# Two half-full key blocks made as one across the array's columns and rows, and a last key moved to VectorE

## The reference, cut to what matters

```python
def _L0_xattn_ref(x, w1, w2):
    h = jnp.einsum('eth,efh->etf', x, w1)
    a = jax.nn.gelu(h, approximate=True)
    return jnp.einsum('etf,efh->eth', a, w2)
...
    x = x + _L0_xattn_ref(_layernorm(x, axis=-1), ctx_1024, ctx_1024)
    x = x + _L0_ffn_ref(_layernorm(x, axis=-1), L0_ffn_Wg, L0_ffn_W1, L0_ffn_W2)
    x = x + _L1_xattn_ref(ctx_1024, _layernorm(x, axis=-1), mask_Bx1x1xS2_bk0, ...)
    x = x + _L1_ffn_ref(_layernorm(x, axis=-1), L1_ffn_Wp1, ...)
```

## Time and profile before

| | |
|---|---|
| median of three runs | 666.88 us (666.12 to 671.56) |
| the profiled execution | 669.96 us |
| its span, first to last instruction | 668.1 us |
| TensorE busy | 619.4 us, 93% of the span |
| VectorE busy | 328.3 us, 49% |
| ScalarE busy | 264.4 us, 40% |
| first matmul of the blocks / end of the last | 13.32 us / 213.8 us |
| mean granted TensorE clock | 0.98 of full speed |

### The profile page before, as it was taken

How to read it: one execution, slowest core, us unless ns; L and a number is a source line. 1 busy time by engine, 2 the same in 40 slices (tenths; PEclk the granted TensorE clock), 3 DMA queues, 4 the chain that set the end, 5 groups by cost and what they waited for, 6 DMA issues and landing times.

```text
span 668.1 us, 9082 instructions
## 1 busy us (share of the span) xinstructions
PE 619.4 (93%) x3053; PEld 381.4 (57%) x3055; DVE 328.3 (49%) x1041; ACT 264.4 (40%) x362; POOL 121.8 (18%) x178
## 2 busy tenths in 40 slices
PE   3999999999999768799999878999999999999998
PEld 1666666666666535699998533334434433336665
DVE  4243330300301687423322967687887887834301
ACT  0211111111111334234442456767676678584321
POOL 0000000000001000254661026230041040043410
PEclk9999998999989899999999979999999999999999
DMA  9992600731400432434223894352551500041141
GB/s 313 358 366 93 206 0 1 253 95 63 130 0 1 150 114 73 131 99 134 95 72 104 237 154 64 41 80 48 104 86 40 98 1 3 2 128 47 41 134 65
DMA packets 50632, 70.53 MB, mean 106 GB/s; under 512 B 7568, under 2 KB 39226, under 8 KB 50186
## 3 DMA queue, kind: packets, MB, share of 16 engines
q1 hardware_dynamic: 48538, 64.45, 35.6%
q0 software_dynamic: 2048, 5.51, 2.8%
HBM read 48.22 MB, written 15.13 MB: 95 GB/s over the span
## 4 chain that ended last, share of the span: by engine, by line
PE 77%; DVE 12%; DMA 4%; issue 3%; ACT 2%; POOL 1%; DVEq 0%; POOLq 0%; ACTq 0%; SPq 0%
PE ps L928 14%; PE ps L939 14%; PE ps L1499 8%; PE ps L1481 6%; PE ps L1388 6%; PE ps L1106 6%; PE ps L1114 5%; PE ps L1225 4%; PE ps L1237 3%; DVE arena L2198 3%; DVE arena L1909 3%; PE ps L1150 2%; PE ps L1411 2%; PE ps L915 1%; DMA arena<-arena 1%
## 5 line engine op out<-in xcount | busy, mean ns | idle before, releaser
L1728 ACT ACTIVATE arena<-ps 100x1024 f32<-100x1024 f32 x128 | 123.9, 1021 | 54.6 <-PE ps L1481 54.4
L2198 DVE TENSOR_REDUCE arena<-ps 128x1 f32<-128x400 f32 x256 | 129.5, 564 | 27.4 <-PE ps L1388 25.6
L928 PE MATMUL ps<-xnT,arena 128*128 128x512 f32 x208 | 101.7, 614 | 0.9 <-DVE xnT L1793 0.9
L1535 ACT ACTIVATE arena<-ps 128x512 f32<-128x512 f32 x52 | 31.1, 597 | 176.0 <-PE ps L928 176.0
L939 PE MATMUL ps<-arena 128*128 128x256 f32 x416 | 100.2, 385 | 0.0
L939 PEld LDWEIGHTS ps<-arena 128*128 128x128 f32 x416 | 80.9, 194 | 33.6 <-issue 24.8
L1388 PE MATMUL ps<-arena 97*128 97x400 bf16 x256 | 75.8, 341 | 3.8 <-DMA arena<-arena 2.3
L1481 PE MATMUL ps<-arena 100*100 100x512 bf16 x256 | 76.2, 381 | 1.9 <-DMA arena<-arena 0.7
L1499 PE MATMUL ps<-arena 100*32 100x512 f32 x512 | 69.1, 604 | 0.0
L1388 PEld LDWEIGHTS ps<-arena 97*128 97x128 bf16 x256 | 20.4, 98 | 75.2 <-DVE arena L2198 47.0
L1793 DVE COPY xnT<-ps 128x512 f32<-128x512 f32 x16 | 10.4, 687 | 100.9 <-PE ps L901 100.9
(11 more groups left out here) (239 smaller groups left out, 688.6 us busy)
## 6 DMA issues: line engine op xcount, KB each, us to landing
arena<-in_W SPq DMA_DIRECT2D x16, 512.0 KB, 9.6
arena<-in_ctxT SPq DMA_DIRECT2D x4, 1664.0 KB, 8.2
arena<-in_ctxN SPq DMA_DIRECT2D x4, 1664.0 KB, 12.6
arena<-arena SPq DMA_DIRECT2D x48, 128.0 KB
last_k_parts<-arena SPq DMA_DIRECT2D x24, 100.0 KB, 1.8
arena<-last_k_parts SPq DMA_DIRECT2D x8, 300.0 KB
x_tok<-in_x SPq DMA_DIRECT2D x4, 512.0 KB, 9.4
xn_rows<-xn SPq DMA_DIRECT2D x4, 512.0 KB
```

The source lines that it names most:

```text
L928: ins = pe.matmul(ps[:, 4 + k % 2, :], ctxT_s[:, b % 2, c, f * P:f * P + P], xnT[:, c, S * b:S * b + S], start=(c == 0), stop=(c == KC - 1))
L1535: act.activation(hid[:, k % 4, :], ps[:, 4 + k % 2, :], ACT.Gelu_apprx_tanh).then_inc(s_a, 1)
L1728: act.activation(pexp2[0:KT, c % 4, :, :], ps[0:KT, 2 + 2 * (c % 2):4 + 2 * (c % 2), :], ACT.Exp).then_inc(f_pe, 1)
L2198: dve.tensor_reduce(nm2[:, m // MU % 2, h, j:j + 1], ps[:, FAST.bank(x), 0:KF], AX.X, ALU.max, negate=True).then_inc(s_by["dve"], 1)
```

## The change

The 65 keys of a batch's rest are split into 64 and one.

- The two rests of 64 keys of batches 0 and 1 become one block of the loop, "rests", and so do those of batches 2 and 3. The loop has 50 blocks instead of 52. The list `BLOCKS` puts the rests of a pair behind the first full block of the odd batch: at places 13 and 38.
- In a rests block the scores are four matmuls of 64 keys by 512 tokens: those of the even batch go to columns 0 to 63 of the array, those of the odd batch to columns 64 to 127. They fill the two halves of one bank of PSUM, so ScalarE activates them with one instruction as before. The values are eight matmuls: four with rows 0 to 63 of the array into the even batch's banks, four with rows 64 to 127 into the odd batch's banks, in turn.
- The 1601st key goes to VectorE: `score_last_key(b)` multiplies the normalized tokens with the key and sums (four instructions for a batch), ScalarE activates 128 by 4 numbers ahead of blocks 11, 12, 24 and 36, and `add_last_key(b)` adds the key times the activated score to `x_tok` (four instructions). SP loads the key of each batch, one row spread over 128 partitions.
- The counts that others wait for are those of the new order (`BLOCKS_OF` = 14, 25, 39, 50 instead of 13, 26, 39, 52), and the steps at 38 and 47 move to 37 and 46.

```diff
+BLOCKS = []
+for _b in range(B):
+    BLOCKS += [("full", _b, _f) for _f in range(FULL)]
+    if _b % 2:
+        BLOCKS.insert(len(BLOCKS) - FULL + 1, ("rests", _b - 1, FULL))
+KEY_AT = (11, 12, 24, 36)
...
+            def load_last_key(b):
+                if b >= 2:
+                    sp.wait_ge(s_res, b - 1)
+                    sp.wait_ge(s_cand, 32 + 16 * b)
+                row = LAST_KEY if b % 2 == 0 else FULL * P
+                sp.dma_start(last_key[:, b % 2, :], a["ctxN"][b, row:row + 1, :].broadcast_to([P, D])).then_inc(s_cand, 16)
...
             load_ctx(1)
+            load_last_key(0)
+            load_last_key(1)
...
             load_ctx(2)
+            load_last_key(2)
             sp.wait_ge(s_mrow, 1)
             sp.dma_start(mask_d, mrow_b[:, :]).then_inc(s_mst, 16)
             load_ctx(3)
+            load_last_key(3)
...
+                        else:
+                            for i in range(2):
+                                ins = pe.matmul(ps[REST * i:REST * i + REST, 4 + k % 2, :], ctxT_s[:, i, c, f * P:f * P + REST],
+                                                xnT[:, c, S * (b + i):S * (b + i) + S], start=(c == 0), stop=(c == KC - 1), tile_position=(0, REST * i))
...
+                        else:
+                            for i in range(2):
+                                lo = REST * i
+                                ins = pe.matmul(ps[:, 2 * i + t // 2, t % 2 * D:t % 2 * D + D], hid[lo:lo + REST, (k - 2) % 4, t * P:t * P + P],
+                                                ctxN_s[lo:lo + REST, i, f, :], start=False, stop=(i == 0), skip_group_check=True, tile_position=(lo, 0))
...
+                if k in KEY_AT:
+                    b = KEY_AT.index(k)
+                    act.wait_ge(s_soft, b + 1)
+                    act.activation(last_a[:, TB * b:TB * b + TB], last_s[:, TB * b:TB * b + TB], ACT.Gelu_apprx_tanh).then_inc(s_exp8, 1)
...
+            def score_last_key(b):
+                dve.wait_ge(s_cand, 32 + 16 * (b + 1 if b >= 2 else 2))
+                dve.wait_ge(s_ln, b + 1)
+                if b:
+                    dve.wait_ge(s_soft, b)
+                for t in range(TB * b, TB * b + TB):
+                    ins = dve.scalar_tensor_tensor(last_prod[:, :], xn[:, t, :], 1.0, last_key[:, b % 2, :], ALU.mult, ALU.mult,
+                                                   accum_out=last_s[:, t:t + 1])
...
+            def add_last_key(b):
+                dve.wait_ge(s_exp8, b + 1)
+                for t in range(TB * b, TB * b + TB):
+                    ins = dve.scalar_tensor_tensor(x_tok[:, t, :], last_key[:, b % 2, :], last_a[:, t:t + 1], x_tok[:, t, :], ALU.mult, ALU.add)
+                ch.step(dve, ins)
...
             take_columns(1)
+            for b in range(2):
+                score_last_key(b)
...
                 if b == 2:
                     mask_any()
                     take_columns(b)
+                    for i in range(2):
+                        add_last_key(i)
...
                 layer_norm(b)
+                if b < 2:
+                    score_last_key(b + 2)
                 take_columns(b)
                 take_logits(b)
+                if b < 2:
+                    add_last_key(b + 2)
```

More of the change, by code:

```diff
@@ L25 @@
 NF = -(-L // P)
+FULL = L // P
+REST = P // 2
+LAST_KEY = FULL * P + REST
+assert LAST_KEY + 1 == L
+BLOCKS = []
[4 more added lines that the diff above has]
+KEY_AT = (11, 12, 24, 36)
+BLOCKS_OF = [max(i for i, x in enumerate(BLOCKS) if x[1] == b or x[0] == "rests" and x[1] + 1 == b) + 1 for b in range(B)]
 E, F = 8, 512
@@ L307, in build @@
         vare = sb("var_eps", [P, NT], F32)
+        last_s = sb("last_key_scores", [P, NT], F32)
+        last_a = sb("last_key_activated", [P, NT], F32)
         rsq = sb("root_squared", [P, NT], F32)
@@ L350, in build @@
         lst3 = view([16, 16])[0:1, :, :]
+        last_key = view([2, D])
         assert at[0] <= W_AT
@@ L920, in _ @@
                 if k < NK:
-                    b, f = divmod(k, NF)
+                    kind, b, f = BLOCKS[k]
                     if f == 0:
@@ L938, in _ @@
                     for t in range(TB):
-                        ins = pe.matmul(ps[:, b % 2 * 2 + t // 2, t % 2 * D:t % 2 * D + D], hid[:, (k - 2) % 4, t * P:t * P + P], ctxN_s[:, b % 2, f, :],
-                                        start=(f == 0 and t % 2 == 0), stop=(f == NF - 1), skip_group_check=True)
+                        if kind == "full":
+                            ins = pe.matmul(ps[:, b % 2 * 2 + t // 2, t % 2 * D:t % 2 * D + D], hid[:, (k - 2) % 4, t * P:t * P + P], ctxN_s[:, b % 2, f, :],
+                                            start=(f == 0 and t % 2 == 0), stop=(b % 2 == 1 and f == FULL - 1), skip_group_check=True)
+                        else:
[3 more added lines that the diff above has]
+                                                ctxN_s[lo:lo + REST, i, f, :], start=False, stop=(i == 0), skip_group_check=True, tile_position=(lo, 0))
                     ins.then_inc(s_mm2, 1)
@@ L2466, in lay_out @@
     ctxN = np.zeros((B, NF * P, D), np.float32)
-    ctxN[:, 0:L, :] = c
+    ctxN[:, 0:FULL * P, :] = c[:, 0:FULL * P, :]
+    for b in range(B):
+        rest, last = (FULL * P, LAST_KEY) if b % 2 == 0 else (FULL * P + REST, FULL * P)
+        ctxN[b, rest:rest + REST, :] = c[b, FULL * P:LAST_KEY, :]
+        ctxN[b, last, :] = c[b, LAST_KEY, :]
     mask = np.zeros((B, LP), np.uint8)
```

41 lines of the change are left out of this document (23 added, 18 removed).

## The result

| | before | after |
|---|---|---|
| median | 669.67 us (20 runs, 666.12 to 671.60) | 665.63 us (20 runs, 661.61 to 668.08) |
| the profiled execution | 669.96 us | 666.83 us |
| its span, first to last instruction | 668.1 us | 665.0 us |
| mean granted TensorE clock | 0.984 | 0.982 |

The account below looks back on a forecast made before the run. TensorE was taken to bound the first attention's loop: -13.76 us for four blocks, + 2 x (1.72 + 1.72) for two rests blocks, + 1.4 for shape changes = -5.5, so 666.88 - 5.5 = 661.4 us, range 659.2 to 665.4.

Parts of the forecast that it names:

- What bounds the kernel: First attention's loop: TensorE sets its time, so a microsecond taken out counts whole; four blocks of 3.44 us save 13.76 us.
- The overlap of halves: Rests blocks: both array halves work at once, 1.72 us each for scores and values, against 3.44 us without overlap.
- the nearer guess: Values of a rests block: 8 rounds, 1.72 us, taken over the upper bound of 16 rounds, 3.44 us.
- The changes of shape: Four rests groups between whole-array groups: 0.35 us each for going in and out, 1.4 us in sum, bounds 0.9 and 1.5.
- The order of the program: the rival: Rests blocks: tiles start only in program order, 0.43 us more for scores, 0.215 for values; 662.7 us, chance 0.12.
- The work put beside: Last key's work on VectorE, ScalarE and SP: all hidden, at nothing; 0.52 us counted per score, keys there by 31 us.
- The base: Whole kernel: the 5.5 us gain was subtracted from the median 666.88 us, giving 661.4 us.
- The clock: Falls behind the router logits: 1.7 us lost each time; a median of few runs can move by one, either way.

Follow-up runs that it names:

- after_dose: The changed kernel with 12 matmuls more at step 30, in the middle of the stage, whose result nobody reads; 672.02 us (12 runs), ratio 1.0026.
- tile_order: The changed kernel with all matmuls of one half of a rests block written before those of the other, instead of in turn; 670.45 us, one execution.
- after_again: The changed kernel run again unchanged, for a second trace and the clock of more executions; 665.93 us (10 runs), ratio 0.9938.
- after_nokey: The changed kernel without loads, scores, activation or additions of the 1601st key, which its result then lacks; 665.11 us (12 runs), ratio 0.9924.
- logits1_at_41: The changed kernel with transposes and logits of batch 1 at step 41 instead of 37, ahead of a full block; 666.02 us (12 runs), ratio 0.9942.
- before_split: The kernel before with router logits of batches 0, 1 and 2 moved a step (batch 1: two) behind their transposes; 663.11 us (6 runs), ratio 0.9893.
- before_split2: The same kernel as before_split, once more on another chip; 661.58 us (6 runs), ratio 0.988.

## Why the prediction was right and where it failed

**What bounds the kernel: right.** The blocks were on the path, and time put into them arrived whole (5.18 us of dose, 6.35 measured, error 0.8).

**The overlap of halves: right, for rows too.** 1.87 and 1.93 us to the next group, where 3.44 would have said no overlap. For the rows the prediction had no row to go by and took the nearer guess, so that part was luck; it holds when the halves stand in turn.

**The changes of shape: right in sum, 1.5 us for 1.4.** The scores cost 0.35 us more than a full block's (0.15 in the group, 0.09 ahead of it, 0.11 behind) and the values 0.40 (0.21, 0.09, 0.10), so 0.75 us for a rests block and 1.5 us for both. The structural gain is then 2 x 3.44 - 1.5 = 5.4 us, for 5.5 forecast. The Trainium skill (TensorEngine Tiling (Array Packing), Key Properties) says that a change of tiling mode drains the engine; by that rule, the trace agrees. It also says there that tiles operate independently, and here too the traces agree, for halves by rows as long as they stand in turn.

**The order of the program: the rival is false, but the order does matter for the values.** Its price was 0.43 us for the scores and 0.215 for the values, if two tiles start only in order. In turn nothing of it shows: the values make eight rounds, although their 1.93 us are the figure that the prediction gave for the rival. Half by half the values take 0.96 us more; starts strictly in order would have made it some 1.5, the 3.4 us of the expectation for `tile_order`. The Trainium skill (TensorE: Matmul & The Clock Gate, Part 3, The mechanism) states that matmuls start and end strictly in the order of the program. By it the scores in `tile_order` would have overlapped less too, since four rows of a half stood together; they took 1.87 us all the same. By that rule, the trace does not agree: the second half's first row starts 0.9 us ahead of the first half's third.

**The work put beside: right.** All of VectorE's, ScalarE's and SP's additions cost nothing. A score took 0.46 us where 0.52 was counted. The first two keys took 10.4 us from issue to landing in the median of the two, and the first score, which waits for both, started without a wait at 34.30 us; the prediction had them there by 31.

**The base: wrong by 2.7 us.** The step was "I forecast the median: 666.88 - 5.5". The median of three was taken as the level of the kernel, although the same paragraph says that the profiled execution was 3.1 us over it. The 82 runs of before have a mean of 669.55. The sum against its own execution, 664.5 us, was in the text and would have missed by 1.1 us. With 669.67 as the base the forecast would have been 664.2 us, and a range as wide around it would have held the result.

**The clock: mis-sized, by 1.4 us.** The step took the falls as noise that is the same for both kernels ("a median of few runs can move by one such drop ... either way"). The structure is worth 5.4 to 5.5 us in every pair of traces that can be compared, and less arrives. The stage by the traces, from the start of the first score to the start of the last row of values:

| falls of the clock in the stage | before's order | after's order |
|---|---|---|
| two | 200.07, 199.84, 199.62 us | 194.22, 194.87 us |
| three | none seen | 195.56, 195.77 us |
| none (waits taken out) | 193.60, 192.98, 192.49 us | 187.11, 186.81, 187.05, 187.87, 187.72 us |

The first rows of the stage, up to the first values, take 6.9 to 8.3 us, and this differs from execution to execution in both kernels. Counted from the first values on, the traces of a kind agree within 0.05 us. With two falls they take 192.32 us in before (three times) and 186.78 and 186.83 in after's order; with none 185.31 (three times) and 179.91 (five times). So the change takes 5.5 and 5.4 us out of the stage. Behind the stage, equal work takes equal time: from the first matmul of the second attention's values (L1536) to the last row of it 192.03 us before and 192.01 after, the experts 72.43 and 72.33. What differs are the places where the clock is low. Behind the experts the final projections of after, in the timeline of TensorE,

```profile
369.89 1.06 PE L1236 MATMUL ps<-cst,xn 128*128 128x128 f32 x8 [1.56 <-DVE xn L1824]
371.74 5.37 PE L1187 MATMUL ps<-xnT,wq 128*128 128x512 f32 x8 [0.79 <-ACT xnT L1729]
```

take 5.37 us, and the same eight rows of before, behind a wait of the same length, 3.67:

```profile
373.27 1.06 PE L1199 MATMUL ps<-cst,xn 128*128 128x128 f32 x8 [1.28 <-DVE xn L1783]
375.12 3.67 PE L1150 MATMUL ps<-xnT,wq 128*128 128x512 f32 x8 [0.78 <-ACT xnT L1688]
```

That stretch, from the last product of the experts to the first maxima (L1425), takes 34.0 us in the three traces of before and 36.67 and 36.08 in the two of after: one fall more, 2 to 2.7 us. In the trace of after the stretch behind it (to the first L1536) had one fall less and gave 1.1 us back, 22.43 for 23.49; in that of `after_again` it did not.

The means of all runs say how much of the missing time this is:

| pair | change | clock lost, before | clock lost, after |
|---|---|---|---|
| as they are (82, 30 runs) | -3.97 us, error 0.37 | 10.8 us, error 0.3 | 11.35, error 0.4 |
| logits a step later (12, 12) | -2.9, error 0.8 | 6.2, error 0.8 | 10.2, error 0.45 |
| and one wait filled (6, 11) | -3.9, error 0.8 | 4.7, error 0.9 | 5.5, error 0.5 |

Among the runs of one kernel, a microsecond more of clock lost makes the time 0.55 us longer (before) or 0.63 (after), probably since part of it falls where TensorE waits. In the middle pair the 4.0 us more of clock lost are then worth some 2.4 us by estimate, which is all that is missing there (5.4 - 2.9 = 2.5, error 0.8). In the first pair the 0.55 us, with an error of 0.5, are worth 0.3 of the missing 1.4.

**What stays open.** That the changed order makes falls more frequent, or puts them at dearer places, is seen in single traces, and is shown by the means in the middle pair alone. Six traces have after's order with its waits (after, `after_again`, `after_nokey`, `after_dose`, `logits1_at_41`, `tile_order`). Four of them have a third fall in the stage, and none of the three of before. Behind the stage five of them take 469.4 to 470.3 us and one (`logits1_at_41`) 467.9, where before takes 467.7 to 468.1. Why, is open: the rests block beside the logits is not the cause, nor the key's work, nor the time at which the stage ends. About 1 us in the first and the third pair is not accounted for; it is less than three standard errors of the first and less than two of the third.

## What to carry to other kernels

Two half-full products of a loop that sets the time can be made as one across the array, by columns and by rows, when their matmuls stand in turn in the program; the price here was 0.35 to 0.40 us for each group of another shape, against 1.72 us saved. Don't let TensorE wait between small pieces of work: moving 8-column products away from their transposes, so that the 0.94 us waits between them went, was worth more (6 to 7 us) than the whole change, and it cost a move by one or two steps. And take the base of a forecast from the execution that the sum was made on, or from many runs: a median of three was 2.7 us off, half of the gain under study.

## What the runs showed of the hardware that was not expected

- The falls of the clock are not noise alone. The three traces of before have them at the same places (110, 195, 230, 281 and 387 us), each at 1.2 GHz, with 1.7 us lost (3.4 at 387 us), around transposes or small products with a wait of 0.9 to 2.6 us. Such a wait is not enough for a fall: the one before 158 us brought none in these three traces. A place can change from one execution to the next (158 and 195 us in the two traces of after).
- Executions of one kernel differ most in their falls: `before_split` in the profiled execution had none in the stage, and falls at five places behind it (218, 228, 276, 371, 385 us), and took 668.19 us, 5 over its median. The trace of `before_split2`, the same kernel, has them at two places (222 and 274 us).
- Two halves by rows, each of eight float32 rows of 256 columns, take 1.93 us in turn and 2.89 us one behind the other, with the second half starting 0.97 us behind the first; two halves by columns, of four rows of 512, take 1.87 us either way.
